# Flamingo block on one core: scores by single pairs, two accumulator banks, four work banks

## The reference

```python
# x: (32, 112, 256), ctx_1024: (32, 375, 256), 16 heads of 64; shift = scale = fside (32, 16)
lat = layernorm(_layernorm(x)) * ln2_w + ln2_b
kv = (layernorm(ctx) * ln1_w + ln1_b) @ Wkv          # k, v: (375, 1024) per batch
q = (lat @ Wq) per head * (1 + scale) + shift
attn = softmax(q k^T / 8); o = (attn v) @ Wout
x = x + tanh(g_xattn) * o
h = bitlinear(_layernorm(x), w1, b1)                 # rmsnorm, rows quantised to 8 bits, weights ternary
x = x + tanh(g_ffn) * bitlinear(gelu(h), w2, b2)     # 1024 hidden
```

## Time and profile before

| | us |
|---|---|
| median of 3 runs | 1130.98 (1130.7 to 1131.45) |
| the profiled execution, its own time | 1132.53 |
| its span, first to last instruction | 1130.7 |
| PE busy | 1067.6 (94%) |
| ACT busy | 970.6 (86%) |
| DVE busy | 945.4 (84%) |
| POOL busy | 776.6 (69%) |
| mean granted clock of PE | 0.981 |

### The profile page before, as it was taken

The page is one execution under the profiler, slowest core; times in us unless marked ns, Lnnn a source line. Parts: engine busy times, 40 slices in busy tenths (PEclk is TensorE's granted clock), DMA queues, the critical chain, the costliest instruction groups (busy, mean ns, idle before and its releaser), DMA issues.

```text
span 1130.7 us, 32113 instructions
## 1 busy us (share of the span) xinstructions
PE 1067.6 (94%) x11900; PEld 733.8 (65%) x11900; DVE 945.4 (84%) x2108; ACT 970.6 (86%) x1864; POOL 776.6 (69%) x839
## 2 busy tenths in 40 slices
PE   2789999999999999999999999999999999999983
PEld 1456666676676676767667666766776676667662
DVE  2688789888889888888988878898888888888984
ACT  4588789999999979999999979999999978999862
POOL 4376667766777777676787766678767767877732
PEclk9799999999999999999999999999999999999986
DMA  8246665676776666679666676756666775765741
GB/s 274 52 95 109 105 103 100 121 117 118 114 138 103 107 117 113 120 110 139 113 101 127 118 116 100 133 112 100 128 109 119 118 136 99 102 127 101 120 107 38
DMA packets 409498, 129.42 MB, mean 114 GB/s; under 512 B 391136, under 2 KB 404192, under 8 KB 409344
## 3 DMA queue, kind: packets, MB, share of 16 engines
q1 hardware_dynamic: 409344, 127.36, 64.2%
HBM read 26.71 MB, written 3.67 MB: 27 GB/s over the span
## 4 chain that ended last, share of the span: by engine, by line
PE 73%; ACT 8%; issue 5%; DMA 4%; DVE 4%; POOL 3%; POOLq 1%; DVEq 1%; SPq 0%; ACTq 0%
PE work L833 15%; PE work L834 15%; PE work L835 15%; PE ps_s L852 10%; DMA pt<-pn 4%; PE ps_o L833 3%; PE ps_o L835 3%; PE ps_o L834 3%; ACT prob L606 2%; PE work L916 2%; PE work L945 2%; ACT q_f L572 2%; PE work L907 2%; PE work L954 2%; ACT L606 2%
## 5 line engine op out<-in xcount | busy, mean ns | idle before, releaser
L447 POOL TENSOR_TENSOR pn<-prob,pn 112x750 f16<-112x750 f32 x256 | 399.3, 1565 | 115.7 <-ACT pn L616 104.6
L606 ACT ACTIVATE prob<-ps_s,neg_max 112x375 f32<-112x375 f32 x512 | 265.2, 573 | 9.0 <-DVE neg_max L748 7.1
L748 DVE TENSOR_REDUCE neg_max<-ps_s 112x2 f32<-112x750 f32 x256 | 237.2, 928 | 24.0 <-PE ps_s L852 24.0
L833 PE MATMUL work<-z,wkv_h 128*128 128x375 f16 x512 | 168.2, 328 | 15.1 <-DVE k_l L673 8.7
L833 PE MATMUL ps_o<-v_h,pt 128*128 128x65 f16 (+1 forms) x1536 | 168.3, 195 | 8.8 <-DMA pt<-pn 5.6
L834 PE MATMUL ps_o<-v_l,pt 128*128 128x65 f16 (+1 forms) x1536 | 168.1, 193 | 0.0
L835 PE MATMUL ps_o<-v_h,pt 128*128 128x65 f16 (+1 forms) x1536 | 168.0, 194 | 0.0
L835 PE MATMUL work<-z,wkv_l 128*128 128x375 f16 x512 | 167.0, 326 | 0.0
L834 PE MATMUL work<-z,wkv_h 128*128 128x375 f16 x512 | 166.9, 326 | 0.0
L529 ACT ACTIVATE k_h<-work 128x375 f16<-128x375 f32 x256 | 121.4, 487 | 50.8 <-PE work L835 45.7
L673 DVE SCALAR_TENSOR_TENSOR k_l<-work,k_h 128x375 f16<-128x375 f32 x256 | 136.0, 540 | 33.6 <-ACT k_h L529 33.5
(11 more groups left out here) (133 smaller groups left out, 2725.1 us busy)
## 6 DMA issues: line engine op xcount, KB each, us to landing
ctx_in<-in_ctx SPq DMA_DIRECT2D x32, 375.0 KB
pt<-pn SPq DMA_TRANSPOSE x256, 3.4
x_in<-in_x SPq DMA_DIRECT2D x32, 112.0 KB, 3.8
x_res<-in_x SPq DMA_DIRECT2D x28, 128.0 KB, 5.2
out<-y SPq DMA_DIRECT2D x28, 128.0 KB, 2.0
stage<-in_wkv SPq DMA_DIRECT2D x2, 1024.0 KB, 9.3
stage<-in_w SPq DMA_DIRECT2D x2, 1024.0 KB, 10.5
stage<-in_wq SPq DMA_DIRECT2D x1, 1024.0 KB, 8.5
```

Of the source, the lines that this page charges most:

```text
L447: g.tensor_tensor(buf[:, 1, :, 0:SK], prob[:, p % 2], buf[:, 0, :, 0:SK], ALU.subtract).then_inc(p_lo, 1)
L606: i = a.activation(prob[:, p % 2, h, :], ps_s[0:SQ, 2 * (p % 2) + h, 0:SK], ACT.Exp, bias=neg_max[:, 2 * (p % 2) + h:2 * (p % 2) + h + 1])
L748: v.tensor_reduce(neg_max[:, 2 * (p % 2):2 * (p % 2) + 2], ps_s[0:SQ, 2 * (p % 2):2 * (p % 2) + 2, 0:SK], X, ALU.max, negate=True).then_in ...
L833: t_.matmul(dst, sh, mh, start=(n == 0), stop=False)
```

## The change

It does six things. (1) `ps_s` has two banks, one pair; S of pair g waits for E of pair g-1; M and E use the same two banks for all pairs. (2) `ps_o` has two banks, eight heads; A of every fourth pair waits for N, and N runs twice a batch over eight heads. (3) `work` has four banks. (4) All orders of all engines are new, with lists of their own for start and end; no two S steps stand side by side. (5) The late weights are a step of SP's order of their own (LW), behind the loads of batch 1; the K weights are split in two halves of columns (WKH0, WKH1, WKL0, WKL1), and Z1 of batch 0 is split by DVE and not POOL. (6) TAIL = 2: the last two tiles are transposed on PE, where it was one. The number of buffers `pt` (6) stays.

```diff
-WORK_BANKS = 3
+WORK_BANKS = 4
 NT = B * SQ // P
 RING = 7 * P
+TAIL = 2
 CAST_ACT = (0, 2, 4, 6)
 ORDER["PE"] = [
-    ("V02", 0), ("V00", 0), ("S0", 0), ("S1", 0), ("V01", 0), ("A5", -1), ("Q1", 0), ("K0", 1),
-    ("S2", 0), ("S3", 0), ("OO0", -1), ("A6", -1), ("K1", 1), ("A7", -1), ("ZX", 1), ("V10", 0),
-    ("V11", 0), ("K2", 1), ("A0", 0), ("S4", 0), ("S5", 0), ("F0", -2), ("K3", 1), ("OO1", -1),
-    ("A1", 0), ("V12", 0), ("F1", -2), ("S6", 0), ("S7", 0), ("F2", -3), ("Z0", 2), ("WO", -1),
-    ("K4", 1), ("A2", 0), ("Q0", 1), ("A3", 0), ("K7", 1), ("K5", 1), ("Z1", 2), ("A4", 0),
-    ("K6", 1),
+    ("S2", 0), ("OO0", -1), ("ZX", 1), ("K2", 1), ("A6", -1), ("A7", -1), ("S3", 0), ("V10", 0),
+    ("F0", -2), ("OO1", -1), ("F1", -2), ("A0", 0), ("S4", 0), ("V12", 0), ("V11", 0), ("A1", 0),
+    ("S5", 0), ("WO", -1), ("K3", 1), ("F2", -3), ("A2", 0), ("Z0", 2), ("S6", 0), ("Q0", 1),
+    ("A3", 0), ("Z1", 2), ("K4", 1), ("V00", 1), ("K5", 1), ("S7", 0), ("K6", 1), ("V01", 1),
+    ("A4", 0), ("S0", 1), ("K7", 1), ("V02", 1), ("A5", 0), ("S1", 1), ("K0", 2), ("K1", 2),
+    ("Q1", 1),
 ]
 FIRST["PE"] = [
...
+    ("Z0", 0), ("Z1", 0), ("ZX", 0), ("K0", 0), ("K3", 0), ("K1", 0), ("K2", 0), ("Q0", 0),
+    ("Z0", 1), ("K5", 0), ("V00", 0), ("Z1", 1), ("K4", 0), ("S0", 0), ("K6", 0), ("V01", 0),
+    ("V02", 0), ("S1", 0), ("K0", 1), ("K7", 0), ("Q1", 0), ("ZX", 1), ("S2", 0), ("K2", 1),
+    ("A0", 0), ("K1", 1), ("V10", 0), ("S3", 0), ("V12", 0), ("K3", 1), ("S4", 0), ("A1", 0),
...
 LAST["PE"] = [
...
-    ("V00", 31), ("WO", 30), ("F0", 29), ("F1", 29), ("V11", 31), ("A0", 31), ("V12", 31), ("V10", 31),
-    ("A1", 31), ("A2", 31), ("A3", 31), ("A4", 31), ("A5", 31), ("F2", 28), ("A6", 31), ("A7", 31),
-    ("OO0", 31), ("OO1", 31), ("F0", 30), ("F1", 30), ("WO", 31), ("F2", 29), ("XT", 31), ("F0", 31),
-    ("F1", 31), ("F2", 30), ("HT", 31), ("F2", 31),
...
+    ("A7", 30), ("V00", 31), ("S3", 31), ("OO1", 30), ("K7", 31), ("F0", 29), ("S4", 31), ("F1", 29),
+    ("WO", 30), ("S5", 31), ("V02", 31), ("F2", 28), ("V10", 31), ("S6", 31), ("V12", 31), ("S7", 31),
+    ("A0", 31), ("A1", 31), ("A2", 31), ("XT", 30), ("A3", 31), ("V11", 31), ("F1", 30), ("F0", 30),
+    ("OO0", 31), ("A4", 31), ("A5", 31), ("A6", 31), ("A7", 31), ("OO1", 31), ("WO", 31), ("F2", 29),
+    ("XT", 31), ("F1", 31), ("F0", 31), ("HT", 30), ("F2", 30), ("HT", 31), ("F2", 31),
 ORDER["ACT"] = [
+    ("ZF1", 1), ("PH6", -1), ("KH5", 0), ("VH00", 0), ("E7", -1), ("KH6", 0), ("VH01", 0), ("HR", -3),
+    ("E0", 0), ("KH7", 0), ("XR", -2), ("PH0", 0), ("VH02", 0), ("KH0", 1), ("E1", 0), ("KH1", 1),
+    ("QF1", 0), ("OH0", -1), ("E2", 0), ("PH2", 0), ("KH2", 1), ("ZXF", 1), ("VH10", 0), ("E3", 0),
+    ("OH1", -1), ("LNW", 2), ("E4", 0), ("VH12", 0), ("VH11", 0), ("GE", -2), ("E5", 0), ("PH4", 0),
+    ("KH3", 1), ("SQ", -2), ("ZF0", 2), ("QF0", 1), ("E6", 0), ("KH4", 1),
 ]
 FIRST["ACT"] = [
...
+    ("WKH0", 0), ("LNW", 0), ("WKH1", 0), ("ZF0", 0), ("ZF1", 0), ("WQH", 0), ("ZXF", 0), ("KH0", 0),
+    ("WVH", 0), ("KH3", 0), ("KH1", 0), ("WOH", 0), ("KH2", 0), ("LNW", 1), ("ZF0", 1), ("QF0", 0),
+    ("ZF1", 1), ("KH5", 0), ("KH4", 0), ("VH00", 0), ("KH6", 0), ("E0", 0), ("TNH", 0), ("VH01", 0),
...
 ORDER["DVE"] = [
+    ("M2", 0), ("PH1", 0), ("XTE", -2), ("OT0", -1), ("N1", -1), ("M3", 0), ("KL2", 1), ("VL10", 0),
+    ("HE0", -2), ("M4", 0), ("HTE", -3), ("OT1", -1), ("HE1", -2), ("PH3", 0), ("VL11", 0), ("VL12", 0),
+    ("M5", 0), ("BA", 3), ("X1", -1), ("HMX", -2), ("YE", -3), ("PH5", 0), ("KL3", 1), ("M6", 0),
+    ("N0", 0), ("XST", -1), ("SC2", -2), ("KL4", 1), ("M7", 0), ("KL5", 1), ("VL00", 1), ("SC1", -1),
+    ("KL6", 1), ("M0", 1), ("PH7", 0), ("BB", 3), ("VL01", 1), ("KL7", 1), ("M1", 1), ("VL02", 1),
+    ("BS", 3), ("KL0", 2), ("KL1", 2),
 ]
 FIRST["DVE"] = [
...
+    ("BA", 0), ("BB", 0), ("BS", 0), ("WKL0", 0), ("WKL1", 0), ("ZS1", 0), ("WQL", 0), ("KL0", 0),
+    ("BA", 1), ("BB", 1), ("BS", 1), ("KL3", 0), ("WVL", 0), ("KL2", 0), ("KL1", 0), ("AS0", 0),
+    ("WOL", 0), ("KL5", 0), ("VL00", 0), ("M0", 0), ("BA", 2), ("KL4", 0), ("KL6", 0), ("BB", 2),
+    ("M1", 0), ("VL01", 0), ("VL02", 0), ("BS", 2), ("KL0", 1), ("KL7", 0), ("PH1", 0), ("M2", 0),
...
 FIRST["SP"] = [
...
-    ("LX", 1), ("LD", 1), ("LD", 2), ("LX", 2), ("T0", 0), ("T1", 0), ("T2", 0), ("LX", 3),
+    ("LX", 1), ("LD", 1), ("LW", 0), ("LD", 2), ("LX", 2), ("T0", 0), ("T1", 0), ("LD", 3),
...
-        ps_s = st.enter_context(nc.psum_tensor("ps_s", [P, 4, HALF], F32))
-        ps_o = st.enter_context(nc.psum_tensor("ps_o", [P, 1, HALF], F32))
+        ps_s = st.enter_context(nc.psum_tensor("ps_s", [P, 2, HALF], F32))
+        ps_o = st.enter_context(nc.psum_tensor("ps_o", [P, 2, HALF], F32))
...
-                if b == 1:
-                    load_late_weights()
...
-                if name == "XD" and b < NT - 1:
+                if name == "XD" and b < NT - TAIL:
                     turn_quantised(b)
-                if name == "HD" and b < NT - 1:
+                if name == "HD" and b < NT - TAIL:
                     turn_hidden(b)
                 if name == "LD":
                     load_context(b)
                 if name == "LX":
...
-                        i = a.activation(prob[:, p % 2, h, :], ps_s[0:SQ, 2 * (p % 2) + h, 0:SK], ACT.Exp, bias=neg_max[:, 2 * (p % 2) + h:2 * (p % 2) + h + 1])
+                        i = a.activation(prob[:, p % 2, h, :], ps_s[0:SQ, h, 0:SK], ACT.Exp, bias=neg_max[:, h:h + 1])
...
+            def split_z_first():
+                dve.wait_ge(evacuated[BANK["Z1", 0]], USE["Z1", 0])
+                v.tensor_copy(z[0][:, 0, 1], zf[:, 1])
+                dve.drain()
+                v.tensor_tensor(z[0][:, 1, 1], zf[:, 1], z[0][:, 0, 1], ALU.subtract).then_inc(z_ready, 1)
+
...
-            def normalise_heads(b, quarter):
-                n, heads = H // 4, ps_o[0:SQ, 0, 0:4 * VW].rearrange("p (h e) -> p h e", e=VW)
-                inv = row_inv[:, n * quarter:n * (quarter + 1)]
-                dve.wait_ge(pv_done, b * PAIRS + 2 * (quarter + 1))
-                v.reciprocal(inv, heads[:, :, DH])
-                dve.drain()
-                v.tensor_tensor(attn[:, quarter * D:(quarter + 1) * D].rearrange("p (h d) -> p h d", d=DH),
-                                heads[:, :, 0:DH], inv.unsqueeze(2).broadcast_to([SQ, n, DH]),
+            def normalise_heads(b, half):
+                n, heads = H // 2, ps_o[0:SQ, :, 0:4 * VW].rearrange("p b (h e) -> p b h e", e=VW)
+                inv = row_inv[:, n * half:n * (half + 1)].rearrange("p (b h) -> p b h", b=2)
+                dve.wait_ge(pv_done, b * PAIRS + 4 * (half + 1))
+                v.reciprocal(inv, heads[:, :, :, DH])
+                dve.drain()
+                v.tensor_tensor(attn[:, half * HALF:(half + 1) * HALF].rearrange("p (b h d) -> p b h d", b=2, d=DH),
+                                heads[:, :, :, 0:DH], inv.unsqueeze(3).broadcast_to([SQ, 2, n // 2, DH]),
                                 ALU.mult).then_inc(o_normed, 1)
 
             def layernorm_stats(b):
...
-                    v.tensor_reduce(neg_max[:, 2 * (p % 2):2 * (p % 2) + 2], ps_s[0:SQ, 2 * (p % 2):2 * (p % 2) + 2, 0:SK], X, ALU.max, negate=True).then_inc(max_ready, 1)
+                    v.tensor_reduce(neg_max[:, :], ps_s[0:SQ, 0:2, 0:SK], X, ALU.max, negate=True).then_inc(max_ready, 1)
...
-                if g > 1:
-                    pe.wait_ge(exp_done, g - 1)
+                if g > 0:
+                    pe.wait_ge(exp_done, g)
...
-                        i = t_.matmul(ps_s[0:SQ, 2 * (p % 2) + h, 0:SK], q[r, p, :], k[r, p, :], start=(n == 0), stop=(n == 2))
+                        i = t_.matmul(ps_s[0:SQ, h, 0:SK], q[r, p, :], k[r, p, :], start=(n == 0), stop=(n == 2))
...
-                if p % 2 == 0 and b * PAIRS + p > 0:
-                    pe.wait_ge(o_normed, 4 * b + p // 2)
+                if p % 4 == 0 and b * PAIRS + p > 0:
+                    pe.wait_ge(o_normed, 2 * b + p // 4)
...
-                    o = ps_o[:, 0, head % 4 * VW:(head % 4 + 1) * VW]
+                    o = ps_o[:, head % 8 // 4, head % 4 * VW:(head % 4 + 1) * VW]
```

More of the change, by code:

```diff
@@ L50 @@
 ORDER["PE"] = [
[6 rows of a table removed]
[6 rows of a table added]
 ]
 FIRST["PE"] = [
[11 rows of a table removed]
[12 rows of a table added]
 ]
 LAST["PE"] = [
[12 rows of a table removed]
[12 rows of a table added]
 ]
 ORDER["ACT"] = [
[5 rows of a table removed]
[5 rows of a table added]
 ]
 FIRST["ACT"] = [
-    ("LNW", 0), ("WKH", 0), ("ZF1", 0), ("ZF0", 0), ("ZXF", 0), ("WQH", 0), ("KH1", 0), ("WVH", 0),
[11 rows of a table removed]
[11 rows of a table added]
 ]
 LAST["ACT"] = [
[11 rows of a table removed]
[11 rows of a table added]
 ]
 ORDER["DVE"] = [
[6 rows of a table removed]
[6 rows of a table added]
 ]
 FIRST["DVE"] = [
[9 rows of a table removed]
[13 rows of a table added]
 ]
 LAST["DVE"] = [
[14 rows of a table removed]
[14 rows of a table added]
 ]
 ORDER["POOL"] = [
```

(48 more changed lines are left out.)

## The result

| | median of 4 | lowest to highest | profiled span | granted clock |
|---|---|---|---|---|
| before | 1130.84 us | 1130.45 to 1131.45 | 1130.7 | 0.981 |
| after | 1210.40 us | 1208.13 to 1214.12 | 1209.4 | 0.975 |

The ratio is 1.0705, interval [1.0683, 1.0727]: 79.6 us more, where 1138 was forecast and the range ended at 1152.

The account below looks back on a forecast made before the run. The bound was taken to be TensorE's matmul slots plus going into and out of score matmuls. 29 - 14 + 8 - 11 - 4 = +8 us on a 1130.7 us span gave a median of 1138 us, range 1127 to 1152.

Parts of the forecast that it names:

- part 3: Middle: each score block waits for the previous pair's reduction and exponential; +8 us, bounds 0 and +30.
- The ring: Score banks of one pair: next block waits for reduction and exponential before it, path 2.8 us against at least 3.4.
- Part 1: TensorE's score matmuls: one pair at a time makes 124 more blocks at 0.235 us each, +29 us.
- Part 2: TensorE's waits for banks: fourth work bank and second accumulator bank give back 0 to 14 us; -14 taken.
- rival (a): Middle: the ring decides, with a wait of 0.8 us in each of 30 batches, 1154 us; chance 0.20.
- Part 4: Start: context of batch 1 loads before the late weights, first score near 34 us; -11 us, bounds -14 and -5.
- Part 5: End: WO directly after OO1, tile 26 turned on TensorE, fewer normalisation waits; -4 us, bounds -8 and 0.

Follow-up runs that it names:

- 1142.2: Changed kernel with T2 ahead of the context's load on SP, and that load cut to 32 of 256 columns: 1142.2 us, ratio 1.0106.
- 1158.4: Changed kernel with T2 issued ahead of the loads of context and residual (LD, RS) on SP: 1158.39 us, ratio 1.0243.
- 1149.3: Changed kernel with two context buffers and the context's load a batch ahead, between T3 and T4 on SP: 1149.32 us, ratio 1.0165.
- 1143.7: Changed kernel, SP's order unchanged, each context load but the first cut to 32 of 256 columns (46.9 of 375 KB): 1143.66 us, ratio 1.0112.
- 0.9914: Kernel before, with only the context of batch 1 loaded ahead of the late weights: 1120.19 us, ratio 0.9914.

## Why the prediction was wrong

**The step that failed** is the last sentence of part 3: "The waits of the A jobs for their DMA turns keep 3 us or more, since the order now puts an A job 3 or 4 pairs behind its score". It counted TensorE's jobs and not the chain of the turn: maximum, exponential, casts, GpSimd's subtraction, then SP's queue with LD's wait in it, then a flight beside the load. For pair 2 the sum was 0.3 to 4.8 us longer than the jobs in batches 2 to 28. The facts were in the trace of before: T2 behind ctx_in at 490.48, its landings of 6.3 to 8.6 us in these batches, and A2's waits of 1.1 to 1.4 us where T2 had only 5.9 to 7.1. The changed order leaves 5.6 to 6.0 us in most batches, as short as in a batch of before that waited. The ring was walked along VectorE and ScalarE, but SP's list was never walked. What the runs showed in place of 3 us: 50.8 us ahead of A2, and 1.5 us for a fall of the clock behind some of the longer waits. Undoing T2's place alone gives 52 us back; with the load small as well, 68.

**Part 1, +29: right.** A single block in the middle of the kernel after takes 0.715 us, as in the earlier trace rows: the last A slot ends at 555.52, the next job starts at 556.23.

```profile
555.49 0.19 PE L847 MATMUL ps_o<-v_h,pt 119*128 119x65 f16 x1
...
555.61 0.37 PE L864 MATMUL ps_s<-k_h,q_h 64*112 64x375 f16 x2
...
556.23 0.28 PE L845 MATMUL work<-wout_h,stage 128*128 128x256 f16 x1
```

The Trainium skill (TensorEngine Tiling, Key Properties) says that a change of tiling mode drains TensorE. The trace agrees that such a change costs, with 0.10 us at each side of a block. With the 166 ns that the Trainium skill gives as the constant part of a lone warm matmul (TensorE: Matmul & The Clock Gate, Single matmul latency), the term would have been 41 us, an estimate from that page, 12 too long.

**Part 2, -14: right way, too large.** Z1 now follows A3 without a gap (0.24 us in the earlier trace rows):

```profile
564.91 0.19 PE L847 MATMUL ps_o<-v_h,pt 119*128 119x65 f16 x1
564.94 0.31 PE L919 MATMUL work<-ident,ctx_n 125*128 125x125 f32 x1
```

In the kernel with T2 first and the small load, 1142.2, the time from S0 of batch 3 to S0 of batch 28 is 848.3 us for 826.4 before, +21.9 in 25 batches. Their 100 splits make 23.5 and the pauses of the ring (part 3) 6.9, so some 8.5 us came back there; all 32 batches would make about 11. The gaps ahead of F are 8 us shorter, but these are mostly the waits of F2 of tiles 25 and 26, 3.4 and 5.5 us, and 3.4 us of them return ahead of XT: that belongs to the end.

**Part 3, +8 for the ring: right in size, in part by luck.** In the middle of the kernel after, the only ring waits of size are the pauses of 0.84 us ahead of S4 in four batches, which lose F0 and F1, forecast at 0.8; rival (a), a wait in each batch, did not come. Where A2 no longer waits (1158.4, 1142.2, 1149.3) a pause of 1.64 us ahead of S6 appears in three batches, which lose WO: the walk had not seen it, and in the kernel after A2's wait hides it. The two together cost some 7.6 us.

**Part 4, -11: right** (10.1 alone, 8.8 undone), though the first score came at 36.46 and not near 34. The late weights are 3.7 MB, not over 4. The first score waited 0.82 us for GpSimd's part of the queries:

```profile
36.46 0.37 PE L864 MATMUL ps_s<-k_h,q_h 64*112 64x375 f16 x2 [0.82 <-POOL q_l L457]
```

**Part 5, -4: half right.** From the last matmul of the last A job (1179.40) to the end are 30.0 us, for 31.6 before and 28 forecast. In other runs with the same lists for the end it is 28.0 to 30.8, so 2 us can't be told here. WO follows OO1 directly in the list but still starts 3.3 us after the last A job, as in the earlier trace rows: F0 and F1 had not held it; the chain N1, OO1 and the two halves of OO1's result does, which VectorE ends.

```profile
1182.71 0.27 PE L845 MATMUL work<-wout_h,stage 128*128 128x256 f16 x1 [1.38 <-DVE stage L773]
```

**The sum without the failed step.** With T2 first and the small load the time is 1142.2 for a forecast of 1138, but that flatters the sum: the small load also shortens the first batches. There the first score comes at 34.13, and S0 of batch 3 96.1 us later; in the kernel with two buffers and LD between T3 and T4 (1149.3), which leaves nothing out and where A2 hardly waits either, it is 37.14 and 99.6. That is 6.5 of the 7.7 us between the two profiled spans. The span of the 1149.3 kernel is 17.4 us longer than before, where +8 was forecast: the start gives 7.3 for 11, batches 3 to 27 cost 23.7 and the last ones before the last A job 3.1, together 26.8 for the +23 of parts 1 to 3, and the end gives 2.2 for 4. So the middle came nearly as forecast, and the sum was some 9 us too low apart from the failed step. What the last batches lose is not traced further.

## What to carry to other kernels

When an edit reorders one engine, walk the chain of each moved operand through every queue to its landing, the DMA issuer's in-order list with its waits included, and compare that time with the new distance, not the number of jobs. Here T2 had 8.6 us from issue to use in most batches and needed some 7; that it waited only in the few batches with less said nothing good of an order that leaves it under 6. A load that nobody waits for is not free: where it stood ahead of a turn with slack, and a batch ahead of its reader, it cost little (1149.3). And undo each part by itself, as here the one good part (the start, 0.9914) lay under a bad one.

## What the runs showed of the hardware

- T2, issued behind a 375 KB load of the same queue, landed in 6.4 to 8.6 us (batches 2 to 28 of the kernel after, median 6.8); issued ahead of the load it took 3.1 (median, 1158.4), and behind a load of 46.9 KB 3.3 (1143.7). The feed-forward's turns went from 2.3 and 3.2 to 5.8 and 5.4 us (medians) when the 375 KB load was put ahead of them.
- Behind eight of 13 waits of TensorE ahead of A2 of 2.1 to 4.8 us the granted clock fell to 1.2 GHz, for 3.4 us in seven cases; behind the other five, of 2.1 to 3.4 us, it did not. Between two like batches a fall cost 1.5 us on top of the wait. At the end of that kernel a fall at 1183.36 also came behind two waits of only 1.3 and 1.6 us.
- Going into and out of score matmuls on 64 rows cost 0.09 to 0.10 us a side at every one of 256 blocks, waits aside, whether the block stood among K, V, A, Q, Z or WO jobs.
